# The high part of x, loaded by a casting DMA on GpSimd's queue instead of copied by ScalarE

## The reference, cut to what matters

```
x_q = einsum('oc,bcn->bno', w_qk, y)            x_k = einsum('oc,bcn->bon', w_qk, x)
x_v = einsum('oc,bcn->bon', w_v, x) + b_v
energy = einsum('bnc,bcm->bnm', x_q, x_k)       attention = softmax(energy, axis=-1)
attention = attention / (1e-07 + attention.sum(axis=1))
x_r = einsum('bcn,bnm->bcm', x_v, attention)
out = x + relu(einsum('oc,bcn->bon', w_t, x - x_r) + b_t)
```

## Time and profile before

| | |
|---|---|
| median of 3 runs | 1848.16 us (1847.73 to 1849.26) |
| span of the profiled execution, first to last instruction | 1846.8 us |
| PE busy | 1841.7 us |
| PEld busy | 1553.5 us |
| DVE busy | 1499.5 us |
| ACT busy | 1310.9 us |
| POOL busy | 788.0 us |
| DMA | 101.92 MB, mean 55 GB/s |

### The profile page before, as it was taken

How to read it: one execution, slowest core, us unless ns; L and a number is a source line. 1 busy time by engine, 2 the same in 40 slices (tenths; PEclk the granted TensorE clock), 3 DMA queues, 4 the chain that set the end, 5 groups by cost and what they waited for, 6 DMA issues and landing times.

```text
span 1846.8 us, 26440 instructions
## 1 busy us (share of the span) xinstructions
PE 1841.7 (100%) x8901; PEld 1553.5 (84%) x8901; DVE 1499.5 (81%) x2034; ACT 1310.9 (71%) x1799; POOL 788.0 (43%) x422
## 2 busy tenths in 40 slices
PE   9999999999999999999999999999999999999999
PEld 8888888888888888888888888888888888888887
DVE  7878787787887877878878788787787877878777
ACT  7767776677666786667776677766677666776665
POOL 5543344432444424444244452444533444334431
PEclk9999999999999999999999999999999999999999
DMA  3201111011110111101111111111011110111101
GB/s 108 68 25 57 58 68 68 23 68 46 68 68 23 68 46 68 68 33 58 46 68 68 48 43 46 68 68 61 30 48 66 68 68 23 64 50 68 68 1 46
DMA packets 34090, 101.92 MB, mean 55 GB/s; under 512 B 4224, under 2 KB 5248, under 8 KB 34048
## 3 DMA queue, kind: packets, MB, share of 16 engines
q1 hardware_dynamic: 33760, 101.07, 15.8%
q10 hardware_dynamic: 288, 0.39, 0.1%
HBM read 67.90 MB, written 33.55 MB: 55 GB/s over the span
## 4 chain that ended last, share of the span: by engine, by line
PE 98%; DVE 1%; ACT 0%; issue 0%; POOL 0%; DVEq 0%; ACTq 0%; POOLq 0%
PE pv L796 37%; PE row_b L691 19%; PE row_a L691 14%; PE pv L768 9%; PE row_b L754 5%; PE row_a L754 5%; PE row_a L745 5%; PE row_b L745 5%; DVE colsum L536 0%; PE pv L898 0%; PE pv L754 0%; PE pv L931 0%; PE pv L902 0%; ACT p_sb L336 0%; DVE z_lo L503 0%
## 5 line engine op out<-in xcount | busy, mean ns | idle before, releaser
L218 POOL TENSOR_TENSOR y_lo<-y_raw,y_hi 128x896 fp32r<-128x896 f32 (+1 forms) x128 | 277.1, 2190 | 546.7 <-ACT y_hi L297 357.1
L543 DVE SCALAR_TENSOR_TENSOR p_lo<-p_sb,row_inv,p_hi 128x1024 fp32r<-128x1024 f32 x254 | 325.4, 1282 | 96.0 <-ACT p_hi L344 95.9
L327 ACT ACTIVATE ev<-row_b 128x512 f32<-128x512 f32 x384 | 229.5, 598 | 199.7 <-PE row_b L691 199.1
L203 POOL TENSOR_TENSOR x_lo<-x_sb,x_hi 128x1024 fp32r<-128x1024 f32 x63 | 152.2, 2415 | 449.2 <-ACT x_hi L280 449.2
L336 ACT ACTIVATE p_sb<-p_sb,neg_max 128x1024 f32<-128x1024 f32 x256 | 295.1, 1154 | 28.6 <-DVE neg_max L518 24.6
L344 ACT ACTIVATE p_hi<-p_sb,row_inv 128x1024 fp32r<-128x1024 f32 x256 | 292.4, 1143 | 30.7 <-PE pv L796 30.0
L536 DVE SCALAR_TENSOR_TENSOR colsum<-p_sb,row_inv,colsum 128x1024 f32<-128x1024 f32 x224 | 291.7, 1302 | 8.5 <-DVE row_inv L526 0.6
L796 PE MATMUL pv<-p_hi,z_hi 128*128 128x512 f32 x1024 | 273.7, 389 | 0.0
L796 PE MATMUL pv<-p_hi,z_lo 128*128 128x512 f32 x1024 | 273.7, 389 | 0.0
L518 DVE CUSTOM_DVE_ANT_0 p_sb<-row_a,ev 128x1024 f32<-128x1024 f32 x128 | 156.6, 1223 | 143.6 <-PE row_a L691 143.6
L796 PE MATMUL pv<-p_lo,z_hi 128*128 128x512 f32 (+1 forms) x1047 | 271.7, 383 | 0.0
(11 more groups left out here) (157 smaller groups left out, 3585.9 us busy)
## 6 DMA issues: line engine op xcount, KB each, us to landing
x_sb<-x SPq DMA_DIRECT2D x64, 512.0 KB, 4.6
out<-res SPq DMA_DIRECT2D x62, 512.0 KB, 3.4
y_raw<-y SPq DMA_DIRECT2D x64, 256.0 KB, 3.7
y_raw<-y SPq DMA_DIRECT2D x32, 512.0 KB, 3.7
out<-res SPq DMA_DIRECT2D x2, 256.0 KB, 2.1
res<-w_qk SPq DMA_DIRECT2D x1, 256.0 KB, 3.0
res<-w_t_T SPq DMA_DIRECT2D x1, 256.0 KB, 6.7
res<-w_v SPq DMA_DIRECT2D x1, 256.0 KB, 7.8
```

Source lines behind the costliest of these rows:

```text
L218: nc.gpsimd.tensor_tensor(y_lo[:, of:, cols], y_raw[:, 1 + of:8, cols], y_hi[:, of:, cols].bitcast(FP32), ALU.subtract).then_inc(y_lo_done, 1)
L327: nc.scalar.activation(ev[:, to, :], bank_b, ACT.Copy, scale=scale).then_inc(b_copied, 1)
L543: nc.vector.scalar_tensor_tensor(out=p_lo[r][:, :], in0=p_sb[r][:, :], scalar=row_inv[:, j:j + 1], in1=p_hi[r][:, :].bitcast(FP32), op0=AL ...
```

## The change

The part `x_hi` of batches 1 to 31 is no longer written by ScalarE from `x_sb`. GpSimd's queue issues two DMAs per batch that read x from HBM once more and write it, cast to fp32r, into `x_hi` (`x_cast_in`). They stand behind the sums over y and ahead of `y_low`, and in all batches but the first behind a wait on `w_done` that ScalarE had before. `x_low` waits for the load, for the cast, and for the second `copy_b` of pair kt + 2, the instruction that stood ahead of `x_high` on ScalarE. Batch 0 still takes its high part from ScalarE.

```diff
+        x_cast = [sem(f"x_cast{kt}") for kt in range(KT)]
...
-            def x_low(b, par, kt):
-                pool.wait_ge(x_hi_done, KT * b + kt + 1)
+            def x_cast_in(b, par, first=False):
+                if not first:
+                    pool.wait_ge(w_done, KT * (b - 1))
+                for kt in range(KT):
+                    pool.dma_start(x_hi[par][:, kt, :], x_dram[b][:, kt, :]).then_inc(x_cast[kt], DMA)
+
+            def x_low(b, par, kt, slot=None):
+                if slot is None:
+                    pool.wait_ge(x_hi_done, KT * b + kt + 1)
+                else:
+                    pool.wait_ge(x_in[kt], DMA * (b + 1))
+                    pool.wait_ge(x_cast[kt], DMA * b)
+                    pool.wait_ge(b_copied, 3 * slot + 2)
...
-            def batch(b, par, last=False):
+            def batch(b, par, first=False, last=False):
                 if not last:
                     y_sums(b + 1)
+                    x_cast_in(b + 1, 1 - par, first)
                     y_low(b + 1, 0)
                     for kt in range(KT):
-                        x_low(b + 1, 1 - par, kt)
+                        x_low(b + 1, 1 - par, kt, NP * b + kt + 2)
...
-            def x_high(b, par, kt, early=False):
+            def x_high(b, par, kt):
                 act.wait_ge(x_in[kt], DMA * (b + 1))
-                if not early:
-                    act.wait_ge(w_done, KT * (b - 1))
...
-                if t >= 2 and not last:
-                    x_high(b + 1, 1 - par, t - 2, early=first)
```

More of the change, by code:

```diff
@@ L259, in _ @@
                                     ALU.subtract).then_inc(wtT_lo_done, 1)
-            run_batches(pool, lambda b: batch(b, 0), lambda b: batch(b, 1), batch,
+            run_batches(pool, lambda b: batch(b, 0, first=True), lambda b: batch(b, 1), batch,
                         lambda b: batch(b, 1, last=True))
@@ L422, in _ @@
             for kt in range(KT):
-                x_high(0, 0, kt, early=True)
+                x_high(0, 0, kt)
             act.wait_ge(y_in, 3 * DMA)
```

## The result

| | before | after |
|---|---|---|
| median of 18 runs each, same chip | 1847.88 us | 1850.8 us (1850.04 to 1852.5) |
| span of the profiled execution | 1846.8 us | 1849.3 us |
| time of the profiled execution | not on record | 1851.1 us |

What follows compares the result with a forecast made beforehand. TensorE was taken to bound the kernel at its own pace. ScalarE, GpSimd and transfers added 0, batch 0 added 0.2 us to the 1848.16 us median: forecast 1848.4 us, own range 1846.5 to 1851, stated range 1845 to 1862.

Steps and rivals of the forecast that it cites:

- TensorE sets the time; ScalarE's copies are worth nothing.: Whole run: removing ScalarE's 62 copies, 65 us of its time, gains 0, since ScalarE waits for TensorE behind them.
- Rival C: TensorE's waits on ScalarE: its relief returns 3.1 us of lost pace and 1.5 us of waits, 1843.8 us; chance 0.04.
- GpSimd's wait and the issues lie in an idle stretch.: GpSimd before `y_low`: waiting for `w_done` and two DMA issues of 1.0 us each fit inside 11.8 us idle, cost 0.
- The transfers are covered.: Casts' loads before `x_low`: likely 16 us of cover, 0.2 us by the upper bound; cost 0.
- Rival B: Casts' transfers: casting at 35 GB/s lands the second 2.2 us late in 31 batches, 1917 us; chance 0.05.
- `x_low` 1 us earlier in the middle batches.: GpSimd's `x_low` starts at 613.53 instead of 614.56, may wait 0.3 us behind VectorE's `p_lo`; cost 0.
- Rival A: VectorE's L536 at 600.04: cast issue holds it, 0.77 us lost in each of 30 batches, 1871 us; chance 0.11.
- I take 0, bound 2.2: Batch 0: one `x_low` moves about 1 us earlier against two `p_lo`; worst is one 2.2 us hold-up, once.
- The runs' median is 1.4 us above that span, and I keep that distance.: Whole run: the median of 1848.16 us lies 1.4 us above the 1846.8 us span, and the forecast keeps that.
- rival D: All batches: casts bring a fixed cost or more 2.2 us collisions, say 0.3 us per batch, 1857 us; chance 0.06.

## Why the prediction was right, and where it was off

The forecast was 1848.4 us with 0.75 on no measurable change; the measured 1850.8 lies at the upper end of its own range (1851). Point by point:

- *TensorE sets the time; ScalarE's copies are worth nothing.* Right. ScalarE's busy time fell by 59 and not 65 us: the copies overlapped their neighbours by 0.1 us each, and the busy time counts a moment once. The idle time before the third `copy_b` of pair 2 became 1.67 us (taken: 1.8). Rival C gave nothing.
- *GpSimd's wait and the issues lie in an idle stretch.* Right. The issues stand 0.6 us after the place taken, 0.55 us each (taken: 1.0, from below 0.4), and `y_low` starts 3.6 us after them. The column sum L545 takes 1301 ns in the mean, and 1302 before.
- *The transfers are covered.* Right. The casts land in 7.7 us and the x loads in 6.6 instead of 4.6; no `x_low` ever waits for one where it is paced. Rival B is out, and so is any price in time of the cast itself.
- *`x_low` 1 us earlier in the middle batches.* Right: 615.58 with a batch that is 1.97 us late is 613.61, against 614.56 before; its 2.50 us hold 0.1 us of waiting behind `p_lo` (taken: 0.3).
- *Rival A.* Its chain and its slack are real, its trigger is not: eight issues in a row hold neither the column sum nor `finish` nor the two `p_lo`.
- *Batch 0: "I take 0, bound 2.2".* This term was mis-sized: it measures 2.06 us in the first turn. The collision was named as "one more hold-up of 2.2 us, once", and just that came. What I didn't do is place it. The start of `x_low` in batch 0 could be worked out from the timeline of before: ScalarE's copy of x starts there, at 51.90, as soon as the second `copy_b` is over, so without it `x_low` moves from 53.04 to about 52, and VectorE has the pair of `p_lo` from 51.09 to 53.57. An instruction that comes inside the first of the two gets in between them. That is a loss of nearly a whole `x_low`, 2.1 us, and no mere chance of one. And VectorE has only 0.17 us of idle time between there and the end of batch 0 in which it could be made good: 15 us later TensorE still pays 1.96 of the 2.13 us.
- *"The runs' median is 1.4 us above that span, and I keep that distance."* The 1.4 us were taken between a median of runs and the span of one execution. Within one execution the distance from span to time is 1.9 us in the kernel before (the median in the rounds of the experiments) and 1.8 us in the kernel after, so it nearly held, and gives 0.1 us back. What moved lies inside the span, behind the last result: 0.9 us. The step that failed is that the sum has no term for the end of the run. The kernel before has a drain on GpSimd too, of 1.40 us, but SP ends 4.2 us behind it; with 62 DMAs it lasts 6.48 us and ends last. It is the small true part of rival D. The traces show it plainly: the six kernels with 60 or 62 DMAs on that queue have tails of 4.0 to 4.2 us, and those with none, 1, 31 or 248 have 3.1 to 3.3. The medians alone don't settle it. The four of the six that lose nothing else lie 0.7 to 1.1 us over before, against 0.1 and 0.6 with 31 and 248 DMAs, but none of their intervals excludes 1, and the kernel with one small cast lies 0.9 us over before without such a tail.

Together 2.06 + 0.9 = 3.0 us, less the 0.1 outside the span, against 2.9 between the medians; that the two agree so closely is partly luck, given the drift of a microsecond between executions.

Luck played a part in the forecast too: its number lies 2.4 us under the measured one, and its own range held it only through the 2.2 us bound on batch 0.

Open: why the drain takes 0.082 us per DMA from 31 to 62 DMAs, long after these have landed, and less with 248. And of the versions tried none beats the kernel before; one cast per batch with the later `x_low` equals it, with ScalarE 3% of the span less busy, which is worth nothing here.

## What to carry to other kernels

Two engines that share a way to memory make the start of an instruction a matter of who is first: when a wait is moved, write down where the released instruction now lands among the *pairs* of the other engine, in the first batch as well as in the middle one, and if it falls inside the first of two, charge its whole length. A wait that looks superfluous for the data may be there for the pacing (37.5 us here); and work taken off an engine that waits for the bottleneck anyway comes back as waiting, microsecond for microsecond. A queue used for the first time can have a cost at the very end, so compare what lies behind the last result, and not only the time of a batch.

## What the runs showed of the hardware

- A GpSimd DMA issue of a 128-row tile takes 0.55 us for 256 or 512 KB, 0.54 for 128 KB, 0.74 for 1 MB in 256 rows, and doesn't disturb a VectorE instruction that reads two SBUF tiles (1.27 to 1.29 us beside 4.50 us of issues).
- Casting fp32 to fp32r in the DMA takes the time of a copy: landing 6.2 against 6.1 us, issue 551 against 548 ns, although the cast makes 8928 packets and the copy 4960, and takes 4.4% of the DMA engines' span against 3.8%.
- GpSimd closes its program with a drain: 1.40 us with no DMA on its queue, 1.50 with one, 3.95 with 31, 6.3 with 60, 6.48 with 62, 4.36 with 248. In the kernel after it began 5.4 us ahead of SP's end (1848.05 - 1842.61), so only one longer than that sets the end.
- Of two starts 0.01 us apart the one that the trace shows first need not be the one that is served first: the column sum at 84.61 waited for the add at 84.62.
